# First x tile ahead in SyncE's queue, conditions by GpSimd's queue, ten zero matmuls instead of twelve, and high-part products first in the opening projection

## The reference

```python
W = weights[condition]
y = jnp.einsum('bct,bcd->bdt', x, W)                  # y: 64 x 64 x 1024
gate_logits = jnp.einsum('bsd,ed->bse', y, gate_w)    # 8 experts
weights, selected = jax.lax.top_k(gate_logits, 2)
weights = jax.nn.softmax(weights, axis=2)
result = jnp.einsum('bsd,od->bso', y, base_w) + base_b
low = jnp.einsum('bsd,erd->ebsr', y, lora_A)
lora_out = jnp.einsum('ebsr,eor,bse->bso', low, lora_B, w_full)
out = x + result + 2.0 * lora_out
```

## Time and profile before

| what | value |
|---|---|
| median of the timed runs | 477.17 us (476.44 to 477.21) |
| profiled execution, its own time | 476.71 us |
| its span | 474.9 us |
| PE busy | 470.1 us, 99% of the span |
| DVE busy | 352.4 us, 74% |
| ACT busy | 158.9 us, 33% |
| POOL busy | 116.8 us, 25% |

### The profile page before, as it was taken

One profiled execution on the slowest core, in us unless ns is written; L12 is line 12 of the kernel. 1 busy time (PEld: TensorE's weight loads), 2 busy tenths in 40 slices (PEclk: granted clock), 3 DMA queues, 4 the chain that ended last, 5 costly groups with the idle time before them and its releaser, 6 DMA issues.

```text
span 474.9 us, 8144 instructions
## 1 busy us (share of the span) xinstructions
PE 470.1 (99%) x2660; PEld 461.7 (97%) x2660; DVE 352.4 (74%) x636; ACT 158.9 (33%) x262; POOL 116.8 (25%) x113
## 2 busy tenths in 40 slices
PE   8999999999999999999999999999999999999997
PEld 8999999999999999999999999999999999999996
DVE  3967969897786967858687686867869587685843
ACT  4733444224233412333223333422333223432300
POOL 2345142040411404123041420414124041310400
PEclk9999999999999999999999999999999999999999
DMA  8966523626265262733625355262743625344202
GB/s 318 413 229 217 194 95 132 226 68 244 86 203 175 115 213 66 248 111 148 222 92 179 110 188 187 90 230 55 245 130 134 221 87 202 112 169 121 90 23 88
DMA packets 49275, 76.91 MB, mean 162 GB/s; under 512 B 13666, under 2 KB 32226, under 8 KB 49250
## 3 DMA queue, kind: packets, MB, share of 16 engines
q1 hardware_dynamic: 37586, 71.88, 43.2%
q10 hardware_dynamic: 11664, 4.72, 3.7%
HBM read 41.98 MB, written 34.60 MB: 161 GB/s over the span
## 4 chain that ended last, share of the span: by engine, by line
PE 99%; DVE 0%; ACT 0%; issue 0%; POOL 0%; POOLq 0%
PE acc L911 50%; PE acc L903 29%; PE acc L949 9%; PE mixed L943 9%; PE acc L1106 1%; PE acc L929 0%; PE mixed L929 0%; DVE y_lo L614 0%; ACT y_hi L467 0%; DVE x_sb L896 0%; POOL y_moved L360 0%; POOLq L1153 0%
## 5 line engine op out<-in xcount | busy, mean ns | idle before, releaser
L386 POOL TENSOR_TENSOR x_sb<-x_sb,bias 128x1024 f32<-128x1024 f32 x32 | 77.1, 2428 | 220.8 <-DVE x_sb L747 181.5
L903 PE MATMUL acc<-r_hi,y_lo 128*128 128x392 f32 x256 | 87.0, 340 | 0.2 <-DVE y_lo L614 0.2
L903 PE MATMUL acc<-r_hi,y_hi 128*128 128x392 f32 x256 | 86.9, 339 | 0.0
L903 PE MATMUL acc<-r_lo,y_hi 128*128 128x392 f32 x256 | 86.6, 339 | 0.0
L911 PE MATMUL acc<-t_lo,s_hi 128*128 128x384 f32 x224 | 74.9, 334 | 0.0
L911 PE MATMUL acc<-t_hi,s_lo 128*128 128x384 f32 x224 | 74.8, 334 | 0.0
L911 PE MATMUL acc<-t_hi,s_hi 128*128 128x384 f32 x224 | 74.8, 334 | 0.0
L911 PE MATMUL acc<-t_lo,y_hi 128*128 128x384 f32 x216 | 72.4, 335 | 0.0
L911 PE MATMUL acc<-t_hi,y_lo 128*128 128x384 f32 x216 | 72.3, 335 | 0.0
L911 PE MATMUL acc<-t_hi,y_hi 128*128 128x384 f32 x216 | 72.2, 334 | 0.0
L655 DVE TENSOR_TENSOR y_lo<-y_turned,y_hi 128x512 fp32r<-128x512 f32 x60 | 46.0, 807 | 24.3 <-ACT y_hi L523 24.1
(11 more groups left out here) (81 smaller groups left out, 744.6 us busy)
## 6 DMA issues: line engine op xcount, KB each, us to landing
x_sb<-in_x SPq DMA_DIRECT2D x32, 512.0 KB, 4.7
out<-x_sb SPq DMA_DIRECT2D x31, 512.0 KB, 3.1
y_scratch<-y_whole SPq DMA_DIRECT2D x60, 256.0 KB, 2.1
y_moved<-y_scratch SPq DMA_DIRECT2D x120, 128.0 KB, 2.8
t_raw<-in_w_quads SPq DMA_DIRECT2D x4, 768.0 KB, 9.2
scratch<-low_turns ACTq DMA_DIRECT2D x16, 128.0 KB, 1.8
low_turns<-scratch ACTq DMA_DIRECT2D x64, 32.0 KB, 2.4
r_raw<-in_w_plain SPq DMA_DIRECT2D x8, 196.0 KB, 5.1
```

The lines of the kernel that those rows point to most:

```text
L386: nc.gpsimd.tensor_tensor(x_sb[:, slot(c), :], x_sb[:, slot(c), :], bias[:, :], ALU.add) \
L903: return nc.tensor.matmul(acc[:, i, 0:NP], y_part[:, i, k, :], w_part[:, k, :], start=(k == 0 and product == 0), stop=(k == KT - 1 and pro ...
```

## The change

Four edits stand in the diff. The DMA of the conditions goes from the head of SP's queue to POOL's queue, behind the first memset. The zero matmuls are ten, not twelve. In `first_step` the first two k blocks are written out in an order in which both products with `y_hi` of block 0 and the high product of block 1 come ahead of the first product that reads `y_lo`. The loop over the other blocks starts at 2 and is otherwise as it was.

```diff
-        WARM = 12
+        WARM = 10
...
-            sp.dma_start(cond_sb[:, :], condition).then_inc(cond_in, 16)
             sp.dma_start(first_x[:, 0, :], x_first_pairs[0]).then_inc(first_in[0], 16)
...
             nc.gpsimd.memset(zeros, 0.0).then_inc(zeros_ready, 1)
+            pool.dma_start(cond_sb[:, :], condition).then_inc(cond_in, 16)
             nc.gpsimd.memset(w_pair, 0.0).then_inc(w_zero, 1)
...
-                for k in range(KT):
+                pe.wait_ge(y_hi_ready, 1)
+                pe.wait_ge(r_hi_ready, 1)
+                plain(0, 0, 0, last=1)
+                pe.wait_ge(r_ready, 1)
+                plain(0, 0, 1, last=1)
+                pe.wait_ge(r_hi_ready, 2)
+                plain(0, 1, 0, last=1)
+                pe.wait_ge(y_ready, 1)
+                plain(0, 0, 2, last=1)
+                plain(0, 1, 2, last=1)
+
+                for k in range(2, KT):
                     pe.wait_ge(r_hi_ready, k + 1)
-                    if k % HALF_K == 0:
-                        pe.wait_ge(y_hi_ready, k // HALF_K + 1)
+                    if k == HALF_K:
+                        pe.wait_ge(y_hi_ready, 2)
                     plain(0, k, 0, last=1)
-                    if k % HALF_K == 0:
-                        pe.wait_ge(y_ready, k // HALF_K + 1)
+                    if k == HALF_K:
+                        pe.wait_ge(y_ready, 2)
                     plain(0, k, 2, last=1)
...
-                    if k > 0:
-                        pe.wait_ge(r_ready, k)
-                        plain(0, k - 1, 1, last=1)
+                    pe.wait_ge(r_ready, k)
+                    plain(0, k - 1, 1, last=1)
```

## The result

The changed kernel took 481.19 us (median of four runs, 480.74 to 481.82) against 477.0 us of the kernel before on the same chip: a ratio of 1.0094 with a 95% interval of 1.008 to 1.0109. I had forecast 476.6 us and a range to 478.3 us. It is slower by 4.2 us, and the profiled execution shows where: its span is 479.3 us against 474.9 us.

A forecast was written before the change was run, and what follows sets the result against it. PE is 99% busy, so only the opening, 1.06 to 9.11 us, can give time. Earlier mixing 0.32 us plus product order 0.22 us make 0.54 us: 477.17 − 0.54 = 476.6 us, range 475.8 to 478.3 us.

The forecast's parts named there:

- What bounds the kernel: Whole span: PE is 99% busy, so only the opening, 1.06 to 9.11 us, can give time, and 0.54 us reaches the end.
- later waits have more, by the empty list: PE's waits after the second pair's y_lo: more slack than the 1.0 us there, against a shift of 0.54 us.
- The conditions by POOL's queue: Opening: conditions land at 2.2 to 4.5 us, nearer the lower end, so no delay to the mixing was counted.
- the break-even: Opening: mixing starting at 6.7 us loses some 0.15 us, products return 0.22 us; 477.1 us, no change.
- x first: Head of SP's queue: x issued 0.40 us earlier; whichever of x and cw goes second lands at 5.3 to 5.7 us.
- the middle of 5.8 us: Start of the first mixing, taken between the ends 5.49 and 6.1 us; it was 6.34 us before.
- Two zeros less: Opening: 0.85 us fewer zeros; with mixing at 5.8 us and the rise at 6.98 us, its first half ends 0.32 us earlier.
- the lost clock: Third rival: PE's hole between zeros and mixing costs the fast clock, loss 2.2 us less 0.54 us, 478.8 us; chance 0.14.
- the second rival, late matrices: Opening: cw or the conditions land late, mixing starts at 6.7 us, 477.1 us, no change; chance 0.19.
- case of a rise before 5.5 us: Opening: zeros would have cost nothing before; effect from 0.4 us of gain to 0.35 us of loss.
- The products with the high part first: First step: two products fill the 8.48 to 9.11 us hole, 0.35 us, of which about 0.22 us is kept.

## Why the prediction was wrong

**What bounds the kernel.** That PE was busy from 9.11 us to the end with one wait was read rightly for delays: all of the 4.4 us arrived at the end. It was read wrongly for gains. An empty list of waits says that nobody is late at the present pace; it doesn't say by how much. I had looked at that room for the first steps only near the opening ("later waits have more, by the empty list"), and this sentence was false: with PE 0.7 us ahead, L949 of the third step waited, and a DMA trip that took 2.6 us instead of 1.7 us was enough for it.

**The conditions by POOL's queue. This is the step that failed:** the sum had no delay for them, and through them the mixing started at 9.00 us, not at 5.8 us. I bounded the landing by 1.2 and 3.5 us after the issue and took the lower end because 256 bytes are little. It was 5.5 us. The upper bound came from a transfer of 32 KB at another time; the row that I had in hand for this place and time was x itself, which had moved nothing for 1.6 us behind `cw`. A small transfer behind or beside large ones paid their time here, not its own. Counted with x's 4.5 us it would have landed at 5.9 us and PE started at 5.9 + 1.3 + 0.4 = 7.6 us, beyond the 6.7 us at which I had put the break-even. Also the issue was later than I put it, 1.35 us instead of 1.00 us, and the register loads and their sequencer work before the copies took 8.50 − 6.89 = 1.6 us, not 1.3 us.

**x first.** I expected 5.3 to 5.7 us for both large transfers. They landed at 6.2 and 6.4 us (5.7 and 5.9 us in the execution with 24 zeros), and in the run with the conditions on ACT's queue at 4.0 and 6.3 us. Taken with the 0.4 us from the landing to the first mixing, the middle of 5.8 us for the mixing was beyond reach in every variant with x first.

**Two zeros less, and the slow rate.** With the conditions at the head, ten zeros and the new order the mixing began at 5.89 us, 0.04 us after x had landed at 5.85 us. But with twelve zeros it began at 5.80 us, so no run shows a gain of the two zeros; what the sum has as 0.32 us would belong to executions in which the rise is as late as 6.98 us. I gave the lost clock 0.14 and tied it to a hole of 0.3 us; the hole was 3.9 us, and the price was 2.07 us in the traces against the run with 24 zeros, 1.3 us by the medians. I priced it at 2.2 us. The way differed: I had let the rise come late, and it had come before the hole and was lost in it. So this rival was right that a hole ahead of the mixing costs the fast clock, but it was not an alternative to the second rival, late matrices; it was its consequence. I added up their chances where one should have carried the other's price: a late start of 2.66 us and slow rows together.

By the Trainium skill ("TensorE: Matmul & The Clock Gate", Part 1: The HAM clock gate) the moment of the rise is not the same in every run. The traces agree: the zero rows began at 1.06 us in all of them, and the rise fell near 7.0 us in the kernel before and before 5 us in the changed one, whose 20 zero rows took 4.00 us instead of 4.5 us. The prediction's case of a rise before 5.5 us, in which the zeros cost nothing, is the traced execution of the new order alone.

**The products with the high part first** filled the hole as they should, and a wait for `r_hi` of block 2 followed, as forecast. But the 0.22 us of the sum were mis-sized: 0.02 us is what came of them by the second pair's mixing (1.79 us instead of 1.81 us). `r_hi` of block 2 was ready at 9.00 us, its product started at 9.05 us, and the next one 0.28 us later instead of 0.177 us, as behind the wait of before (9.11 to 9.40 us).

What stays open: why two queues together moved less from 1.9 to 3.5 us than one alone, why the store of `low_turns` took 0.9 us longer in one execution, and what part of a time difference of 0.5 us between executions is due to the moment of the rise. That the medians with ten zeros and the new order show no gain is measured; that DVE and the DMA trips take it in the median execution too is argued from two slow ones. Whether the new opening would pay with more room on DVE was not shown; the two ways I tried to make room were worse.

## What to carry to other kernels

A transfer of a few bytes that others wait for belongs ahead of the bulk on all queues. In these runs neither a queue of its own nor the second place behind a large transfer saved it from traffic that had been issued before. Price it by what is in flight at that moment, not by its size.

When two inputs are needed together, the later one sets the time: moving one ahead of the other only exchanges them. When a wait may open a hole on TensorE near the start, add the price of the slow rate to it from the outset, and keep the zeros long enough to cover the latest plausible landing. And before a few rows less are counted as a gain, compare executions: the moment of the rise moved this opening by some 0.8 us between two executions.

A kernel that is 99% busy passes every delay to its end, but not every gain. Before counting one, measure the room of the waits behind it, over the first steps where constants are still prepared, and see whether the engine that is waited for moves along.

## What the runs showed that I had not expected

- 256 bytes landed 1.8 us after their issue by POOL's queue with all else quiet, 5.5 us (5.2 us in one execution) beside two transfers of 512 KB; on SP's queue behind x it was 5.1 us.
- Two queues with 512 KB each, issued together at 0.80 us, landed at 6.2 and 6.4 us, or at 5.7 and 5.9 us in another execution. With 0.4 us between the issues (the kernel before) the first one landed at 4.4 us and the second at 5.7 us, with 0.56 us (the conditions in ACT's queue) at 4.0 and 6.3 us.
- A hole of 3.0 us on PE was enough to bring the clock down to 1.2 GHz once it had risen; holes of 0.53 us (24 zeros) and 0.65 us (T4's low part moved, ten zeros) left the rows fast.
- DVE's subtraction of 128x1536 took 3.95 us beside POOL's addition and 1.75 us alone; one of 128x256 took 2.34 us and 0.43 us.
- The clock column can read 1.00 where the rows are slow, at the start of a trace and until the first rise: with the conditions in ACT's queue it did so up to 10 us. Later in the changed kernel it read 0.50 for the same rate.
